# One chip, five attention layers: a bias add moved to the head of GpSimd's unit, the last projection split at its seventh pair, one row fill at another slot

## The reference

```python
x = _L0_xattn_ref(x, ctx, maskB, ...)   # cross attention with a mask per batch, then MLP
x = _L1_xattn_ref(x, ctx, maskS, ...)   # cross attention, self attention (masked), then MLP
x = _L2_xattn_ref(x, ctx, ...)          # causal self attention, cross attention, then MLP
x = _L3_xattn_ref(x, ctx, ...)          # RMS norm, cross attention with heads of 64
...
h = _attn(q, memory, ...)               # softmax(q k^T * scale + mask) v, then @ ow + ob
x = queries + h
```

## Time and profile before

| what | before |
|---|---|
| median of 3 runs | 5001.2 us |
| the profiled execution, its time | 5001.92 us |
| its span on the core | 5000.1 us |
| PE busy | 4638.2 us (93%), 24484 matmuls |
| DVE busy | 3055.2 us (61%) |
| ACT busy | 2305.5 us (46%) |
| POOL busy | 1061.3 us (21%) |
| granted clock of TensorE, mean | 0.985 |

### The profile page before, as it was taken

How to read it: one execution, slowest core, us unless ns; L and a number is a source line. 1 busy time by engine, 2 the same in 40 slices (tenths; PEclk the granted TensorE clock), 3 DMA queues, 4 the chain that set the end, 5 groups by cost and what they waited for, 6 DMA issues and landing times.

```text
span 5000.1 us, 66240 instructions
## 1 busy us (share of the span) xinstructions
PE 4638.2 (93%) x24484; PEld 1873.6 (37%) x24484; DVE 3055.2 (61%) x7970; ACT 2305.5 (46%) x3011; POOL 1061.3 (21%) x991
## 2 busy tenths in 40 slices
PE   7999999989998999999899988899989999999999
PEld 2333333333332333433444433334333333333333
DVE  6777776557677777666466675555524455454554
ACT  4455554466654444444444555444443333333332
POOL 0112221111111111111111111111113333333333
PEclk9999999999999999999999999999999999999999
DMA  1111111121111110011111211111120000000000
GB/s 60 35 59 49 46 41 42 39 88 58 64 62 46 38 37 33 31 35 51 63 61 61 70 59 52 35 37 35 45 71 22 13 1 13 13 13 13 1 13 9
DMA packets 164465, 201.67 MB, mean 40 GB/s; under 512 B 36273, under 2 KB 119601, under 8 KB 162866
## 3 DMA queue, kind: packets, MB, share of 16 engines
q1 hardware_dynamic: 141106, 176.34, 10.5%
q0 software_dynamic: 23040, 21.10, 1.7%
HBM read 128.86 MB, written 68.42 MB: 39 GB/s over the span
## 4 chain that ended last, share of the span: by engine, by line
PE 60%; issue 19%; DVE 13%; ACT 4%; DMA 2%; POOL 1%; SPq 0%; DVEq 0%; POOLq 0%; ACTq 0%
PE psO L722 8%; PE small L651 7%; PE small L658 6%; PE psT L697 6%; PE psT L927 5%; PE psS L679 4%; DVE nmb L1172 4%; PE psT L780 3%; PE psT L651 2%; PE psT L887 2%; PE psO L942 2%; PE psT L897 2%; PE psT L942 2%; ACT probs L992 2%; DVE nmb L1169 2%
## 5 line engine op out<-in xcount | busy, mean ns | idle before, releaser
L992 ACT ACTIVATE probs<-psT 128x1024 f32<-128x1024 f32 (+3 forms) x1280 | 1160.0, 961 | 1269.6 <-PE psT L697 1076.9
L1172 DVE TENSOR_REDUCE nmb<-psS 128x1 bf16<-128x512 f32 x1024 | 649.7, 685 | 282.5 <-PE psS L679 282.4
L1169 DVE CUSTOM_DVE_ANT_0 out<-psS,pens_sb 128x512 f32<-128x512 f32 x1024 | 665.2, 685 | 236.7 <-issue 235.5
L697 PE MATMUL psT<-low 32*128 32x512 f32 (+3 forms) x5120 | 748.1, 605 | 25.4 <-ACT probs L992 22.3
L679 PE MATMUL psS<-out 32*128 32x512 bf16 (+3 forms) x2560 | 597.0, 377 | 119.6 <-DVE nmb L1169 58.0
L722 PE MATMUL psO<-probs,V 128*32 128x512 f32 (+3 forms) x5120 | 655.3, 584 | 18.0 <-DVE probs L1181 11.8
L1355 DVE TENSOR_REDUCE parts<-psS 128x2 bf16<-128x1024 f32 x256 | 314.9, 1230 | 531.3 <-PE psS L914 531.3
L1098 ACT ACTIVATE probs<-psT 128x1024 f32<-128x1024 f32 x256 | 262.0, 1023 | 524.9 <-PE psT L930 524.9
L679 PEld LDWEIGHTS psS<-out 32*128 32x128 bf16 x2560 | 149.9, 91 | 816.5 <-issue 439.7
L780 PE MATMUL psT<-out,W 128*128 128x512 f32 x768 | 383.0, 621 | 0.4
L1022 ACT ACTIVATE low<-small,vec 128x256 f32<-128x256 f32 (+1 forms) x464 | 261.9, 616 | 230.4 <-PE small L651 230.2
(11 more groups left out here) (178 smaller groups left out, 5770.4 us busy)
## 6 DMA issues: line engine op xcount, KB each, us to landing
o_mid<-out SPq DMA_DIRECT2D x160, 256.0 KB, 2.0
oN<-o_mid POOLq DMA_DIRECT2D x160, 128.0 KB, 3.5
oN<-r_mid SPq DMA_DIRECT2D x80, 256.0 KB
x_mid<-xe SPq DMA_DIRECT2D x40, 512.0 KB, 2.9
xw<-x_mid SPq DMA_DIRECT2D x36, 512.0 KB, 4.0
xe<-x_mid SPq DMA_DIRECT2D x36, 512.0 KB, 4.9
cT<-ctxT SPq DMA_DIRECT2D x20, 512.0 KB, 5.6
W<-wm SPq DMA_DIRECT2D x6, 1024.0 KB, 8.5
```

Source lines behind the costliest of these rows:

```text
L697: last = nc.tensor.matmul(psT[j][:, q0:S], Kf[rows_of(j), q, a, c, kt * P:(kt + 1) * P], Qf[rows_of(j), q, a, c, q0:S], start=True, stop=p ...
L992: nc.scalar.activation(probs[:, i % 2, two, q0:S], psT_all[:, two, q0:S], ACT.Exp, scale=float(DH) ** -0.5)\
L1169: nc.vector.tensor_tensor_reduce(junk[:, e, 0:n], psS[e][:, 0:n], penalty, 1.0, -3.0e38, ALU.add, ALU.max, at).then_inc(sem[f"s_read{e}"], 1)
L1172: nc.vector.tensor_reduce(at, psS[e][:, 0:n], AX, ALU.max).then_inc(sem[f"s_read{e}"], 1)
```

## The change

Three edits:

1. `bias_x(o_row)` with its two waits (for `xe` and for the weights' bias row) becomes the first thing of a unit's list on GpSimd, ahead of `rsqrt(nxt)` and the gather.
2. The last batch's four projection tiles no longer go through the two banks of `tail_fill`. They get four banks. Their first seven head pairs (28 matmuls) stand right behind the fill of `s63`; the eighth pair's four matmuls follow the wait for the last scaled output. SP stores each token tile by itself, 128 KB each, instead of 512 KB at once.
3. `m0` moves from slot 24 to 25 in turns with an MLP, and from slot 26 to 24 in the others, ahead of `k10` at 25.

```diff
--- before.py
+++ after.py
@@ -76,8 +76,8 @@
 Y_USES = {True: uses_at("10 y01, 12 y23"), False: uses_at("14 y0, 15 y1, 17 y2, 19 y3")}
 MLP_USES = uses_at("18 h0, 19 h1")
 CTX_USES = {True: uses_at("13 c0, 14 c1"), False: uses_at("10 c0 c1")}
-NXT_USES = {True: uses_at("6 x0, 7 x1, 9 q0, 16 k0, 21 q1, 23 k1, 24 m0, 27 v0, 29 v1"),
-            False: uses_at("6 x0, 7 x1, 9 q00, 10 q01, 11 k00, 13 k01, 21 q10, 23 q11, 25 k10, 26 m0, 27 k11, 29 v0, 31 v1")}
+NXT_USES = {True: uses_at("6 x0, 7 x1, 9 q0, 16 k0, 21 q1, 23 k1, 25 m0, 27 v0, 29 v1"),
+            False: uses_at("6 x0, 7 x1, 9 q00, 10 q01, 11 k00, 13 k01, 21 q10, 23 q11, 24 m0, 25 k10, 27 k11, 29 v0, 31 v1")}
 COUNT_USES = uses_at("30 w")
 MASKS_AT = (3, 5, 7)
 
@@ -178,7 +178,7 @@
 TAIL_MIXED = len(TAIL_FIRST) - 1
 TAIL_EARLY = TAIL_MIXED - 3
 TAIL_TURNS = {5: TAIL_FIRST[:TAIL_EARLY], 7: TAIL_FIRST[TAIL_EARLY:TAIL_MIXED]}
-TAIL_END = [f"s{PAIRS - 1}"] + [f"y{B - 1}_{t}" for t in range(T)]
+TAIL_END = [f"s{PAIRS - 1}"]
 TAIL = TAIL_FIRST + [name for at in range(PAIRS * T) for name in tail_extras(*divmod(at, T))] + TAIL_END
 TAIL_AT = {name: i for i, name in enumerate(TAIL)}
 assert len(TAIL_AT) == len(TAIL)
@@ -329,6 +329,8 @@
         tail_summed = semaphore("tail_summed")
         tail_o_scaled = semaphore("tail_o_scaled")
         out_stored = semaphore("out_stored")
+        last_full = semaphore("last_full")
+        last_read = semaphore("last_read")
 
         def count(name, u, k):
 
@@ -485,6 +487,7 @@
         psO5 = [psO[:], psT[2]]
         tail_small = [small[:], psT[3]]
         tail_mixed = [psS[0], psT[3]]
+        last_banks = [tail_small[(TAIL_AT[TAIL_END[0]] + 1) % 2], psS[0], psS[1], psT[0]]
 
         block = stack.enter_context(nc.Block())
 
@@ -633,10 +636,10 @@
                 name = f"y{b - 1}_{T - 1}"
                 sp.wait_ge(tail_small_read[tail_bank(name)], tail_fills(name) + 2)
                 sp.dma_start(tokens(out[b - 1]), x5[(b - 1) % 2][:]).then_inc(out_stored, 16)
-            name = f"y{B - 1}_{T - 1}"
-            sp.wait_ge(tail_small_read[tail_bank(name)], tail_fills(name) + 2)
-            sp.dma_start(tokens(out[B - 1]), x5[(B - 1) % 2][:]).then_inc(out_stored, 16)
-            sp.wait_ge(out_stored, 16 * B)
+            for t in range(T):
+                sp.wait_ge(last_read, t + 1)
+                sp.dma_start(out[B - 1, t * P:(t + 1) * P, :], x5[(B - 1) % 2][:, t, :]).then_inc(out_stored, 16)
+            sp.wait_ge(out_stored, 16 * (B - 1 + T))
 
 
         @block.tensor
@@ -975,8 +978,24 @@
                             pe.wait_ge(tail_small_read[tail_bank(name)], tail_fills(name) + 2)
                     tail_outputs(at - 1)
             tail_outputs(T * PAIRS - 1)
-            for name in TAIL_END:
-                tail_fill(name)
+            tail_fill(TAIL_END[0])
+
+            def last_tile(t, pairs):
+                for m in pairs:
+                    last = nc.tensor.matmul(last_banks[t][:, 0:D], o5[(B - 1) % 2][m][:, t * P:(t + 1) * P], Wo5[:, m, :],
+                                            start=m == 0, stop=m == NP - 1)
+                return last
+
+            name = TAIL[-2]
+            pe.wait_ge(tail_small_read[tail_bank(name)], tail_fills(name) + 2)
+            pe.wait_ge(tail_s_read, T * PAIRS)
+            pe.wait_ge(tail_exp_done, T * PAIRS)
+            pe.wait_ge(tail_o_scaled, PAIRS - 1)
+            for t in range(T):
+                last_tile(t, range(NP - 1))
+            pe.wait_ge(tail_o_scaled, PAIRS)
+            for t in range(T):
+                last_tile(t, range(NP - 1, NP)).then_inc(last_full, 1)
 
 
         @block.scalar
@@ -1405,8 +1424,11 @@
                     tail_moments_of(b + 1)
                 if m == 4 and kt == 2 and b + 1 < B:
                     tail_normalise(b + 1)
-            for name in TAIL_END:
-                tail_take(name)
+            tail_take(TAIL_END[0])
+            for t in range(T):
+                dve.wait_ge(last_full, t + 1)
+                xs = x5[(B - 1) % 2][:, t, :]
+                nc.vector.tensor_tensor(xs, xs, last_banks[t][:, 0:D], ALU.add).then_inc(last_read, 1)
 
 
         @block.gpsimd
@@ -1454,14 +1476,14 @@
                 nc.gpsimd.tensor_tensor(oC, oC, rB, ALU.mult).then_inc(sem["o_scaled"], 1)
 
             def body(place, prev, cur, nxt):
+                if prev is not None:
+                    pool.wait_ge(sem["xe_in"], count("xe_in", prev, 16))
+                    pool.wait_ge(wo_in, 16 * (prev.s + 1))
+                    bias_x(o_row).then_inc(sem["biased"], 1)
                 if nxt is not None:
                     rsqrt(nxt, 1)
                 if prev is not None:
                     gather_outputs(place, prev)
-                if prev is not None:
-                    pool.wait_ge(sem["xe_in"], count("xe_in", prev, 16))
-                    pool.wait_ge(wo_in, 16 * (prev.s + 1))
-                    bias_x(o_row).then_inc(sem["biased"], 1)
                 if prev is not None:
                     scale(prev)
                 if nxt is not None and nxt.s == 0:
```

## The result

The changed kernel takes 4929.07 us (median of 4 runs, 4919.61 to 4936.24) beside 5003.51 us for the kernel before (median of 4), measured with it. The ratio is 0.9846, 95% interval 0.9819 to 0.9872: 1.5% faster. In a later batch of five runs the same kernel took 4932.39 us, ratio 0.9841 (0.9812 to 0.9869). The forecast was 4927 us. Two runs further down, one with the m fill alone (5834.90 us, granted clock 0.74) and one with parts 1 and 2 (5043.84 us, 0.94), fell into a slow state, and the ratios leave them out.

What follows compares the result with a forecast made beforehand. PE, busy 93% of the span, was taken to wait on DVE, whose normalising GpSimd's bias adds hold. Moving the adds 61, the end 6.9 and m0 7.6 sum to 75 us off 5001.9: 4927 us forecast, range 4903 to 4958.

Steps and rivals of the forecast that it cites:

- The cause: DVE's two-tile normalising: GpSimd's bias adds, not the gather's issue, stretch it, 3.18 us against 0.73.
- Stage 3: Stage 3's turns: moving the adds saves 26 us, stall and slow clock together; 15 with the clock still falling.
- The turn that nature gave: A stage 3 turn whose normalising missed the adds: 20.36 us against 25.01 over the same stretch, 4.65 us a turn.
- Stage 4: Stage 4, path from DVE's reciprocals to the first y fill: the whole normalising excess comes back, 14.9 us.
- m0: Moved m0 fill: 3.4 us in stage 4, 1.4 in stages 0 and 2, 2.8 without MLP; 7.6 us in all.
- more comes back: Rival, chance 0.08: stage 4's y fills at full clock, 5 x 1.6 us, and the same at stage starts; 4912 us.
- Stages 0 and 2: Stages 0 and 2: 0.9 of 17.3 us excess, plus 2 for a min beside the adds; 17.6 us, bounds 9 and 19.
- nearly all passes on: Stages 0 and 2: with PE one pair ahead of DVE, 0.9 of DVE's 17.3 us excess shortens the time, 15.6 us.
- half of DVE's time is slack elsewhere: Rival, chance 0.09: another wait ends last; stages 0 to 2 give half, stage 3 keeps its slow clock; 4950 us.
- Stage 1: Stage 1: half of DVE's 10.7 us excess comes back, since some lies in the first two tiles and stays; 5.5 us.
- The new place: Slots 27 to 31, where the adds go: a loss of 3 us to the min of stages 0 and 2, bounds 0 and 31.
- The end: Last batch's projection: 28 matmuls without a pause, last add 6.1 us sooner, smaller last store 0.8; 6.9 us, 5.5 to 7.7.

Runs made afterwards that it cites:

- parts 1 and 2: The changed kernel with m0 back at its old slots in all turns: 4939.85 us, ratio 0.9828; 5043.84 us in a slow state.
- the stall without GpSimd: The changed kernel with a DVE reciprocal, its result unread, in slot 4 of six turns of stage 3: 4970.22 us, ratio 0.9913.
- GpSimd's memsets: The changed kernel with four memsets of an unread spare tile behind the gather, where the bias adds used to stand: 4938.45 us, ratio 0.985.

## Why the prediction was right

The sum was made against the profiled execution: 75 us forecast, 82.3 measured. In the order of its steps:

- **The cause** is right. All 58 us of DVE's excess left with the adds, and adds on a spare tile bring 3.18 us back. As a whole part 1 was put at 61 us; measured alone it gave 47 to 77.
- **Stage 3**, 26 us: 28.8 measured with part 3's share. The turn that nature gave, was worth 4.65 us a turn in the forecast; alone, the moved adds give 64.9 - 60.2 = 4.7. The second half of it, the clock, is shown by the stall without GpSimd.
- **Stage 4**, 14.9 us and 3.4 for m0: 18.0 in this execution. The sum is met, not each term. The wait of the first y fill has gone from 4.20 us to between 0.4 and 1.5 in four of its turns, and the fill keeps its clock:

```profile
3472.36 1.97 PE L661 MATMUL small<-Wo,oN 128*128 128x256 f32 x8 [0.54 <-POOL oN L1476]
```

It had 3.58 us in the earlier trace rows. This is what the rival "more comes back" named, and it did come here. But the m0 term failed, and the clock falls at another place of the same turn:

```profile
3129.54 0.39 PE L682 MATMUL psS<-out 32*128 32x512 bf16 x2 [0.96 <-ACT out L1045]
...
3132.64 0.39 PE L682 MATMUL psS<-out 32*128 32x512 bf16 x1 [0.95 <-DVE nmb L1191]
...
3135.25 1.93 PE L725 MATMUL psO<-probs,V 128*32 128x512 f32 x8
```

```profile
3132.00:3134.00 2.00, 1.15 (x9) 0.65 (x11) 2.00 (x4) 0.00 (x0) 0.00 (x0) 0.93 0.60 169
3134.00:3136.00 2.00, 2.00 (x14) 0.30 (x9) 1.03 (x3) 1.06 (x2) 0.00 (x0) 0.50 0.98 331
3136.00:3138.00 2.00, 2.00 (x12) 0.68 (x4) 0.64 (x2) 0.88 (x1) 0.23 (x1) 0.72 0.44 155
```

The last rows give PE, PEld, DVE, ACT and POOL busy, then the clock: 0.50 at 3134, after pauses of 0.96 and 0.95 us, and the outputs take 1.93 us where they take 1.06 elsewhere in the turn. These three windows lose 2 x (0.07 + 0.50 + 0.28) = 1.7 us, and the timeline shows such a fall in each of six turns. The 4.20 us shrank by more than DVE's time: counted from the m1 fill, the reciprocals start 8.5 us on for 11.1, 2.6 sooner as forecast, but the scaling ends 19.0 us on for 22.9, 3.9 sooner. The rest lies on the way between them, the store and the load, which takes 9.4 to 12.3 us from turn to turn in these traces. The prediction took it as fixed.
- **Stages 0 and 2**, 17.6 us and 1.4: 4.2 + 9.9 = 14.1. In stage 2 a plain turn gained 1.1 us, about what was taken. In stage 0 it gained 0.2. The step that failed is "nearly all passes on": DVE is early now, and in stage 0 the x fill waits for ACT instead.

```profile
389.04 0.73 DVE L1168 TENSOR_SCALAR xn<-xw,mom,rstd 128x256 f32<-128x256 f32 x2
389.60 1.93 ACT L1052 ACTIVATE pens_sb<-out 128x2048 bf16<-128x2048 uint8 x1
...
394.18 0.63 PE L649 MATMUL small<-ident,xn 128*128 128x128 f32 x4 [1.05 <-ACT hT L1033]
```

ACT makes the next turn's penalties out of its masks just then (1.93 us), its take of the first x tiles comes behind that, and PE's second x fill behind the take. The tiles were ready at 389.77, 4.4 us before they are used. This is the rival "half of DVE's time is slack elsewhere", true of stage 0 and, as the next item shows, of the plain turns of stage 1.
- **Stage 1**, 5.5 us and a share of part 3: 14.1. A plain turn gained 0.8 us, of which 0.6 come from the adds; with five of them that is 4.0 us. The other 10 lie in the first two turns and the last, and 6.5 of the 14.1 are clock. The half was taken because the first tiles' excess would stay, and that is wrong: all 10.7 us of DVE's excess went, the first tiles' too. Of the 1.4 us that DVE has back in a plain turn, 0.6 reached the turn. So the term was mis-sized, and the half came near for plain turns for another reason than the one given. What shortened the first turns beside the clock was not settled.
- **The new place**, -3 us: nothing was lost to the min. In stages 0 and 2 its line takes 304.78 us for 241 in place of 309.02 for 242, so its excess over 1.22 us each went from 13.8 to 10.8 us. The 3.17 us of the earlier trace rows belong to a min that starts together with the adds, and none did in the changed kernel; the longest that an add held one was 0.4 us. That it never came to that is in part luck: the prediction had 0.3 us of margin on either side and could not tell.
- **The end**, 6.9 us: 6.9, and 6.3 alone. 28 + 4 matmuls at 0.43 us came as counted, the last add starts 5.9 us sooner (6.1 forecast), and from its end to the end of the span it is 4917.8 - 4915.49 = 2.3 us in place of 3.3: 1.0 for the small store, where 0.8 was taken.
- **m0**, 7.6 us: the total can't be told from the scatter, and its parts were wrong. Turns with an MLP gave nothing, since the pair put ahead needs k1 too; that could be read off the order of the fills. Turns without gave more in stage 3, 0.8 us a turn for the 0.2 taken, and 0.2 in stage 1.

So the terms were off by up to 7 us each and cancel in part: the 7 us by which the profiled execution beat the sum are those of stage 1, and the -3 of the new place makes up for what stages 0 and 2 gave less. The median came out only 2 us from the forecast because it lies 9.5 us above that execution (4919.61), as the clock varies from run to run: a second profiled execution of the same kernel has 8.5 us more in stage 4. Agreement within 2 us is luck; 10 us is what the method can claim.

## What to carry to other kernels

When an operation takes several times its usual length in some turns, look in the timeline for what the neighbouring engine does exactly then, and for a turn in which the two miss each other: that turn gives the price of the whole stall, the clock's part too, before anything is built. Moving short work of a half-idle engine to where its neighbour does something else cost nothing here and gave 1.5%. A fill moved ahead of another gains nothing when both wait for the same release; follow what each needs, and not only where it stands.

## What the runs showed of the hardware

A pause of PE of 2.4 us cost 5.4 us a turn, since the granted clock was 0.50 (1.2 GHz) for some 9 us behind it though PE was busy throughout. Pauses of 0.95 to 0.99 us were followed by 0.50 in some turns, for 3 to 7 us, and in others by none.

A burst of four adds holds a DVE tile that starts up to 0.3 us ahead of it: the tile ends 0.16 us behind the third add, the next one 0.16 us behind the fourth. GpSimd's memsets, 0.27 us each and reading nothing, hold it for their whole burst in stage 3, but in five turns of stage 4 the tiles pass in 0.41 and 0.47 us and it is the memsets that take longer. A DVE min with two inputs in SBUF ends 1.08 to 1.10 us behind the operation of GpSimd that it found running, be it an add of 0.7 us or a multiply of 2.36, and the next add waits for it (2.8 to 3.8 us for four). The Trainium skill, page "SBUF — State Buffer", section "Who interferes with whom", has both sorts contend and the first to start keep the ports for its whole instruction; the min agrees with that, and that a tile stands back for three adds in a row is more than it states.
